# Side jobs of an attention loop in pieces over all its tiles, two quads of heads in one output bank, and a shorter count of chosen experts

## What is computed

```python
def attention(x):                       # 16 heads of 8
    q = x @ Wq;  latent = (x @ Wk + x @ Wv) @ W_down_kv          # latent: 32
    k = latent @ W_up_k;  v = latent @ W_up_v
    s = clip(q @ k.T / sqrt(128)) * exp(-1e-4 * abs(i - j))      # per head
    return (softmax(clip(s)) @ v) @ Wo
def experts(x):                         # 8 experts, the best 2 of each token, and a shared one
    top_logits, top_idx = top_k(x @ w_router, 2)
    moe = sum over the 2 chosen e: softmax(top_logits)[e] * (silu(proj_e) * gate_e) @ fc2_w[e],
          [proj_e, gate_e] = split(x @ fc1_w[e])
    return moe + (silu(x @ gate_w) * (x @ up_w)) @ down_w
x = layernorm(x + attention(x));  x = layernorm(x + experts(x))
```

## Time and profile before

| | us |
|---|---|
| median of 3 runs | 778.3 (775.71 to 781.35) |
| the profiled execution | 780.54 |
| its span, from first to last instruction | 778.4 |

### The profile page before, as it was taken

How to read it: one execution, slowest core, us unless ns; L and a number is a source line. 1 busy time by engine, 2 the same in 40 slices (tenths; PEclk the granted TensorE clock), 3 DMA queues, 4 the chain that set the end, 5 groups by cost and what they waited for, 6 DMA issues and landing times.

```text
span 778.4 us, 12970 instructions
## 1 busy us (share of the span) xinstructions
PE 658.6 (85%) x4815; PEld 296.5 (38%) x4815; DVE 316.5 (41%) x958; ACT 546.6 (70%) x634; POOL 281.0 (36%) x266
## 2 busy tenths in 40 slices
PE   5029899999999999999999998999999869958850
PEld 2013233333333333333333332333333869846530
DVE  1913332444334344433454442432435323236672
ACT  2028798998989899898889986899997224324222
POOL 1900450550333054033205643312101560267772
PEclk9658899999999999999899998999999989979995
DMA  3699564284255228425522855322243686873221
GB/s 114 214 326 395 190 218 174 96 297 176 96 190 187 99 101 311 157 95 190 189 82 96 314 194 195 131 82 96 100 145 119 204 247 195 265 217 101 67 73 49
DMA packets 76915, 132.04 MB, mean 170 GB/s; under 512 B 6512, under 2 KB 51888, under 8 KB 76848
## 3 DMA queue, kind: packets, MB, share of 16 engines
q1 hardware_dynamic: 72736, 123.63, 46.4%
q0 software_dynamic: 3584, 7.35, 3.1%
q10 hardware_dynamic: 528, 0.18, 0.1%
HBM read 82.38 MB, written 50.33 MB: 170 GB/s over the span
## 4 chain that ended last, share of the span: by engine, by line
PE 69%; DVE 11%; ACT 7%; DMA 4%; issue 3%; POOL 2%; another core or an unknown queue 1%; SPq 0%; ACTq 0%; DVEq 0%; POOLq 0%
PE ps L822 26%; PE ps L809 18%; ACT probs L704 7%; PE ps L980 5%; PE ps L764 5%; PE ps L975 4%; DVE ps L1288 3%; PE ps L989 2%; PE ps L844 2%; DMA queries<-stack_dram 2%; PE ps L868 1%; DVE small L1161 1%; DVE osb L1292 1%; PE ps L991 1%
## 5 line engine op out<-in xcount | busy, mean ns | idle before, releaser
L704 ACT ACTIVATE probs<-ps 128x1024 f32<-128x1024 f32 x512 | 482.4, 1038 | 94.2 <-DVE ps L1288 76.6
L822 PE MATMUL ps<-probs,V 128*9 128x512 f32 x2048 | 274.4, 609 | 0.8 <-ACT probs L704 0.5
L809 PE MATMUL ps<-queries,keys 32*128 32x512 f32 (+3 forms) x1408 | 194.5, 418 | 48.4 <-DMA queries<-stack_dram 31.9
L809 PEld LDWEIGHTS ps<-queries,keys 32*128 32x128 f32 x1408 | 95.0, 187 | 209.0 <-ACT probs L704 133.1
L1288 DVE TENSOR_TENSOR ps<-ps,cpk 128x256 f32<-128x256 f32 x256 | 101.8, 428 | 162.4 <-PE ps L809 154.6
L533 POOL TENSOR_TENSOR stage<-qk,rows_sb 128x512 fp32r<-128x512 f32 x28 | 36.8, 1315 | 169.0 <-DVE qk L1149 153.7
L573 POOL DMA_INDIRECT sorted_dram<-xn,slots x56 | 54.9, 980 | 73.2 <-ACT probs L704 35.5
L585 POOL DMA_INDIRECT queries<-result_dram,slots x56 | 57.3, 1023 | 45.4 <-PE ps L994 25.1
L733 ACT ACTIVATE probs<-ps 128x512 f32<-128x512 f32 x42 | 24.8, 599 | 40.4 <-PE ps L980 26.1
L822 PEld LDWEIGHTS ps<-probs,V 128*9 128x9 f32 x2048 | 30.5, 88 | 57.6 <-issue 43.2
L1391 DVE TENSOR_TENSOR probs<-probs,ps 128x512 f32<-128x512 f32 x42 | 28.4, 685 | 56.6 <-PE ps L975 16.3
(11 more groups left out here) (165 smaller groups left out, 586.2 us busy)
## 6 DMA issues: line engine op xcount, KB each, us to landing
stack_dram<-stage SPq DMA_DIRECT2D x64, 512.0 KB, 6.0
keys<-stack_dram SPq DMA_DIRECT2D x32, 1024.0 KB
queries<-stack_dram SPq DMA_DIRECT2D x32, 512.0 KB
keys<-expert_dram SPq DMA_DIRECT2D x36, 192.0 KB
sorted_dram<-y_pre SPq DMA_DIRECT2D x1, 4608.0 KB, 20.6
result_dram<-probs SPq DMA_DIRECT2D x18, 256.0 KB
rows_sb<-expert_dram SPq DMA_DIRECT2D x20, 192.0 KB
V<-expert_dram SPq DMA_DIRECT2D x16, 192.0 KB
```

Of the source, the lines that this page charges most:

```text
L704: nc.scalar.activation(probs[:, m % 3, 2 * j:2 * j + 2, :], ps[:, 2 * s:2 * s + 2, :], ACT.Exp, scale=SCALE).then_inc(exp_done, 1)
L809: last = mm(bank[2 * s + i][:, lo:hi], keys[rows, u, kt // CT, v, tok(kt % CT)], queries[rows, u, v, lo:hi], start=True, stop=True)
L822: last = mm(bank[OUT_BANK][32 * i:32 * i + HD + 1, :], V[:, c // 2 % 2, kt, 4 * (Q % QUADS) + i, :], probs[:, m % 3, i, :], start=(kt == 0 ...
```

## The change

`side_places` puts the jobs anew, over crossing tiles too, and a job can have one to four parts; each part does its share of the columns or of the 128-token tiles. One `o` job serves two quads, so there are two a chunk, and `evacuate` comes every 16 tiles. To make that possible V holds, for a pair of heads of two quads, `[v_a 1 | zeros | v_b 1]` of 9 columns each, and the outputs take 18 of these 27: the first quad of a pair adds zeros to the second's rows, and the second adds zeros to the first's. `quad(Q)` orders the quads 0, 2, 1, 3. The layer norm's statistics are in two steps (`aggregate` two tiles later). `cnt` takes running sums that VectorE makes (`choose`), with two matmuls instead of five. The other steps of the router follow `wo`, `lg` and `cnt` by a count of tiles.

```diff
             d, p = c - 1, c + 2
-            z = 0 if c % 2 else 4
-            places = {("xT", p): (0 if c % 2 else 2,), ("o", 4 * d + 3): (z + (1 if c % 2 else 0),),
-                      ("q", p): (z + 2, z + 3) if c % 2 else (z + 1, z + 2), ("a", d): (6 if c % 2 else 7,),
-                      ("k", p): (z + 8, z + 9), ("wo", d): (z + 10, z + 11), ("o", 4 * c): (z + 13,),
-                      ("x", d): (z + 16,), ("norm", p): (z + 17,), ("lg", d): (z + 18, z + 19), ("o", 4 * c + 1): (z + 21,),
-                      ("cnt", d): (z + 24,), ("v", p): (z + 25, z + 26), ("o", 4 * c + 2): (z + 27,)}
+            if c == NCH - 1:
+                places = {("o", 2 * d + 1): (1,), ("a", d): (4,), ("wo", d): (7, 8), ("x", d): (14,), ("lg", d): (16, 17),
+                          ("o", 2 * c): (18, 19), ("cnt", d): (22,)}
+            elif c % 2:
+                places = {("xT", p): (0,), ("o", 2 * d + 1): (1,), ("q", p): (4, 5, 6), ("a", d): (7, 8), ("k", p): (9,),
+                          ("wo", d): (13, 14), ("v", p): (15, 16), ("o", 2 * c): (19, 20), ("x", d): (22,),
+                          ("lg", d): (23, 24), ("norm", p): (26, 27), ("cnt", d): (29,)}
+            else:
+                places = {("o", 2 * d + 1): (1, 2), ("xT", p): (3, 4), ("q", p): (5,), ("a", d): (7, 8), ("k", p): (10, 11),
+                          ("wo", d): (12, 13), ("v", p): (16, 17, 18, 19), ("o", 2 * c): (20, 21), ("x", d): (23, 24),
+                          ("lg", d): (26,), ("norm", p): (27, 28), ("cnt", d): (30,)}
             if c == 0:
-                places.update({("norm", 0): (14,), ("norm", 1): (15,)})
+                places.update({("norm", 0): (13,), ("norm", 1): (14,)})
...
             def outputs(m):
                 Q, c, kt = m // NT, m // TPC, m % NT
+                half, k = Q % 2, quad(Q) % 2 * 4
...
-                if kt == 0 and Q:
-                    pe.wait_ge(o_evacuated, Q)
+                if kt == 0 and half == 0 and Q:
+                    pe.wait_ge(o_evacuated, Q // 2)
                 pe.wait_ge(exp_done, 2 * m + 2)
                 for i in range(4):
-                    last = mm(bank[OUT_BANK][32 * i:32 * i + HD + 1, :], V[:, c // 2 % 2, kt, 4 * (Q % QUADS) + i, :],
-                              probs[:, m % 3, i, :], start=(kt == 0), stop=(kt == NT - 1))
+                    last = mm(bank[OUT_BANK][32 * i:32 * i + 2 * (HD + 1), :],
+                              V[:, c // 2 % 2, kt, k + i, half * (HD + 1):(half + 2) * (HD + 1)], probs[:, m % 3, i, :],
+                              start=(kt == 0 and half == 0), stop=(kt == NT - 1 and half == 1))
...
                     elif what == "cnt":
-                        count_chosen(k)
+                        pe.wait_ge(chosen_ready, k + 1)
+                        mm(dst[:, 0:E], before, running[:, CT, :], start=True, stop=True)
+                        last = mm(dst[:, E:2 * E], all_ones, running[:, CT, :], start=True, stop=True)
...
             def keep_values(p, src):
-                rest(copy(V[:, p // 2 % 2, CT * (p % 2):CT * (p % 2 + 1), :, 0:HD],
-                          src.rearrange("r (t h d) -> r t h d", t=CT, h=HEADS)))
+                for half in range(2):
+                    rest(copy(V[:, p // 2 % 2, CT * (p % 2):CT * (p % 2 + 1), :, 2 * half * (HD + 1):2 * half * (HD + 1) + HD],
+                              src.rearrange("r (t w k d) -> r w t k d", t=CT, w=2, k=HEADS // 2)[:, half]))
...
             def choose(d):
-                tt(chosen[:, 0:CT, :], onehot[:, 0, d, :, :], onehot[:, 1, d, :, :], ALU.add).then_inc(chosen_ready, 1)
+                link(tt(running[:, 1:CT + 1, :], onehot[:, 0, d, :, :], onehot[:, 1, d, :, :], ALU.add))
+                for t in range(2, CT):
+                    link(tt(running[:, t, :], running[:, t, :], running[:, t - 1, :], ALU.add))
+                tt(running[:, CT, :], running[:, CT, :], running[:, CT - 1, :], ALU.add).then_inc(chosen_ready, 1)
...
-            def evacuate(Q):
-                dve.wait_ge(pv_done, NT * (Q + 1))
-                copy(osb[:, Q % 2, :], bank[OUT_BANK]).then_inc(o_evacuated, 1)
+            def evacuate(R):
+                dve.wait_ge(pv_done, 2 * NT * (R + 1))
+                copy(osb[:, R % 2, :], bank[OUT_BANK]).then_inc(o_evacuated, 1)
...
-                        statistics(y_pre[:, :], stats, mv, var, var_ready)
+                        for i in range(CT):
+                            rest(nc.vector.bn_stats(stats[:, i, :], y_pre[:, tok(i)]))
...
+                    if since["wo"] == 2:
+                        dve.wait_ge(dve_chain, links[0])
+                        aggregate(stats, mv, var, var_ready)
+                    if since["lg"] == 2:
+                        route_lanes(d)
+                    if since["lg"] == 3 and d < GROUP:
+                        choose(d)
```

More of the change, by code:

```diff
@@ L337, in block_kernel, with quad @@
         assert at[0] <= small.shape[1], at[0]
+        def quad(Q):
+            return (0, 2, 1, 3)[Q % QUADS]
         def stack_rows(n, p, i):
@@ L760, in _, with turn @@
             mm = nc.tensor.matmul
-            def turn(dst, src):
-                for t in range(CT):
+            def turn(dst, src, tiles=range(CT)):
+                for t in tiles:
                     last = nc.tensor.transpose(dst[:, tok(t)], src[:, tok(t)], ident)
@@ L896, in beside @@
                     what, k = name
-                    part = at_tiles.index(t)
-                    halves = range(2 * part, 2 * part + 2)
+                    part, n = at_tiles.index(t), len(at_tiles)
+                    tiles, cols = range(CT * part // n, CT * (part + 1) // n), slice(HALF * part // n, HALF * (part + 1) // n)
+                    dst = bank[SIDE_BANK] if part else side(name)
                     if what == "xT":
-                        turn_x(k)
+                        pe.wait_ge(x_loaded[k % 2], 16 * (k // 2 + 1))
+                        last = turn(dst, x_tok[:, k % 2, :], tiles)
@@ L901, in beside @@
                     elif what == "o":
-                        turn_output(side(name), k).then_inc(side_ready, 1)
-                    elif what in ("q", "k"):
-                        project(k, "qk".index(what), part)
+                        pe.wait_ge(o_evacuated, k + 1)
+                        last = turn(dst, osb[:, k % 2, :], tiles)
+                    elif what == "q":
+                        last = mm(dst[:, cols], Wq_sb[:, :], xT[:, k % 2, cols], start=True, stop=True)
+                    elif what == "k":
+                        last = mm(dst[:, cols], wfold[:, 2, :], xT[:, k % 2, cols], start=True, stop=True)
+                    elif what == "v":
+                        for i in tiles:
+                            last = mm(dst[:, tok(i)], xT[:, k % 2, tok(i)], wfold[:, 3, :], start=True, stop=True)
@@ L905, in beside @@
                     elif what == "a":
-                        turn(side(name), a_tok[:, k % 2, :]).then_inc(side_ready, 1)
+                        last = turn(dst, a_tok[:, k % 2, :], tiles)
                     elif what == "wo":
                         pe.wait_ge(s_wo, 32)
-                        last = out_project(bank[SIDE_BANK] if part else side(name), halves)
-                        if part:
-                            last.then_inc(side_ready, 1)
-                    elif what == "v":
-                        values(k, part)
+                        last = out_project(dst, tiles)
@@ L914, in beside @@
                     elif what == "x":
-                        dst = side(name)
                         pe.wait_ge(xn_ready, k + 1)
-                        turn(dst, xn[:, k, :]).then_inc(side_ready, 1)
+                        last = turn(dst, xn[:, k, :], tiles)
                     elif what == "norm":
-                        norms(k)
+                        pe.wait_ge(squared, k + 1)
+                        for i in range(2 * part // n, 2 * (part + 1) // n):
+                            last = mm(dst[32 * i:32 * i + 32, :], head_sum_h[:, :], squares[:, i, :], start=True, stop=True)
@@ L1168, in statistics @@
                 ts(v, m[:, :, 1], EPS, None, ALU.add).then_inc(s, 1)
+            def statistics(src, st, m, v, s, negated=None):
+                for t in range(CT):
+                    last = nc.vector.bn_stats(st[:, t, :], src[:, tok(t)])
+                link(last)
+                aggregate(st, m, v, s, negated)
             def normal_rows(dst, src, m, r):
```

126 lines of the change are left out of this document (48 added, 78 removed).

## The result

| | before | after |
|---|---|---|
| median, us | 778.66 (775.71 to 781.35) | 749.38 (748.8 to 752.01), 4 runs |
| ratio after / before, 95% | | 0.963 (0.960 to 0.966) |
| the profiled execution, us | 780.54 | 748.8 |
| its span, us | 778.4 | 746.7 |

The kernel is 3.7% faster: 29 us, where 39 were forecast. The same view by stretches as in the earlier trace rows, of the kernel after: chunks 0, 3, 4, 5, 6, then all after attention. The columns are the stretch and its length, the busy time of PE, PEld, DVE, ACT and POOL (with the instructions), the granted clock, the DMA share and GB/s.

What follows compares the result with a forecast made beforehand. ScalarE's exponentials set the free pace, with gaps where TensorE's or VectorE's side jobs delay them. Chunks summed to 498.8 us, plus 4.5 for wide outputs, 503.3 against 542.6: -39.3, so 739.0 us; own range 731 to 750, overall 722 to 762.

Steps and rivals of the forecast that it cites:

- Free pace and floor: Attention: ScalarE needs 0.917 us an exponential, 58.7 a chunk; a middle chunk of 67.8 loses 9.1 in gaps.
- 3.5 of losses: Odd chunks: waits expected to stay around side jobs and crossing tiles, 3.5 us on the floor, giving 62.2.
- TensorE's total of 57.7: TensorE's work in a chunk falls from 59.1 to about 57.7 us, under ScalarE's 58.7.
- Middle chunks: Odd chunks 1, 3, 5 take 62.2 us and even chunks 2, 4 take 62.0.
- The wider outputs, +4.5: Attention outputs: 18 columns of V for 9 cost 0.035 us in half of all tiles, +4.5 us.
- Chunk 0: Chunk 0 takes 67.0 us for 69.2, with the wait of about 4 us for the second `norm` kept.
- Queues that are moved past: GpSimd and SyncE behind `wo`: the next chunk's load goes out at 52 us and lands in time at 6.0.
- Instructions late again: Rival: VectorE's wait of 4.41 us comes again with half clock behind it, +6, 745 us; chance 0.12.
- Load late: Rival: the next chunk's load is 1.8 us late at three boundaries, +5.5, 745 us; chance 0.10.
- Crossing tiles cost more: Rival: pieces ahead of crossing scores cost 0.55 us each, not 0.25; +17, 756 us; chance 0.18.
- TensorE fits under: Rival: TensorE's total fits under ScalarE's and halves of the losses stay; -13, 726 us; chance 0.10.
- wide outputs slow: Rival: 18-column outputs lengthen tiles, at +0.25 us a tile 803 us, slower than before; chance 0.05.

Runs made afterwards that it cites:

- n_count5: `p_norm` with the count of chosen experts as before the change, five matmuls and one short VectorE operation instead of four; 736.43 us, ratio 0.947.
- o_stats: The changed kernel with every job in its old place and the aggregate straight behind `bn_stats` again; 766.45 us, ratio 0.985.
- p_wide32: `a_paced` with the outputs' stationary operand 32 columns wide instead of 18; 741.46 us, ratio 0.955.
- a_paced: The changed kernel with the first group's 32 row sends on GpSimd one a tile, from the start of chunk 6; 739.63 us, ratio 0.953.
- p_norm: `a_paced` with chunk 0's first two `norm` jobs at tiles 2 and 6 instead of 13 and 14; 734.27 us, ratio 0.944.
- a_again: The changed kernel run once more, unchanged; 747.54 us, ratio 0.963.
- b_burst: The kernel before the change with its row sends of chunks 5 and 6 no longer paced by the exponentials; 804.8 us, ratio 1.036.

## Why the prediction was right in part, point by point

The change is 29.3 us faster by the two medians; 39.3 was forecast. Of the 10.4 us between 749.38 and 739.0, 2.8 are how the two profiled executions lie in their runs (2.2 above the median before, 0.6 below it after); the spans account for the other 7.6 (746.7 for 739.1): chunks 5 and 6 +11.3, after attention +1.6, chunk 0 -1.1, the outputs' term -4.5, other chunks and rounding about +0.3. That 749.38 lies within the forecast's own range of 731 to 750 is luck: that range was made for wide outputs and for losses, and a stall that it did not hold filled it.

- **Free pace and floor.** Held for what it was used for: ScalarE's gaps were the loss, and they closed. The floor of 58.7 was not reached: the merged groups above give 60.5, 1.8 us more, and the gaps listed there add 1.5 where the sum had 3.5 of losses. The two errors met, so that the chunks came out right is luck in part.
- **TensorE's total of 57.7.** Its terms held where they have rows: turns gone, and the short count worth 0.65 a chunk against the 0.75 of the sum (`n_count5`).
- **Middle chunks.** 62.0 and 62.2 forecast; 61.72, 61.72, 62.42, 62.70 measured. The largest single losses named there, 1.37 at the end of a quad and 0.84 behind the statistics, went as said; the latter was costed at under 1 us a chunk and is worth 7.3 in all in the old places (`o_stats`): 0.6 in each of chunks 3, 5 and 7, where the clock stayed full, and 1.4 to 3.2 in the others of chunks 1 to 6, half-clock stretches in `o_stats` included.
- **The wider outputs, +4.5.** Mis-sized. The upper bound, 0.035 us a tile, was charged in half of the tiles. The loads grew by 4.1 us in all, even less than 256 x 0.035 = 9, and outputs from start to start stayed at 0.97 to 0.99; `p_wide32` adds 14 columns for 1.8 us by the medians, so nine cost about 1 (an estimate; no run has the change at 9 columns). The term should have been nothing to one. `a_paced` is the kernel that the sum described: its chunks add up to 500.4 where the sum had 498.8 without the term and 503.3 with it, and chunk 5's 63.65 for 62.2 is its largest miss. That its median of 739.63 meets the forecast's 739.0 owes something to this term's error, and to a before of 777.2 in its series where the forecast started from 778.3.
- **Chunk 0.** 65.90 for 67.0: the wait for the second `norm` stayed, as said. It was in reach all the time: 4.6 us by `p_norm`.
- **Queues that are moved past.** This is the step that failed. It followed what stands behind `wo` on GpSimd and SyncE, and not what stands behind `lg`: `gap_power` and, behind it, 12 sends whose gates were set for a `lg` at tiles 18 and 19. The step even gave the rule, to cost each queue that a job is moved past, and left one out. Chunks 5 and 6 were forecast at 122.9 and took 134.2; 124.2 with the sends apart.
- **Instructions late again (0.12, 745).** Its effect came, a stall of 6.3 us with a half clock behind it, above its price (10 us by the traces of after and `a_paced`, 8 by the medians of the pair, for 6). Its mechanism was wrong: not an accident that the change shifts, but a run of GpSimd's DMAs (`a_again`, `a_paced`, `b_burst`), behind which TensorE's signal is late and not VectorE's instruction. The wait of the earlier trace rows fits it (a late signal behind four sends 1.28 us apart, gone when the sends moved in `b_burst`), but no run takes those four sends apart alone.
- **Load late (0.10).** Came in small: at the end of chunk 0, 2.6 us in `a_paced`, and in after 1.01 us at the start of chunk 4 (TensorE's timeline above). It is not what made the miss.
- **Crossing tiles cost more (0.18), TensorE fits under (0.10), wide outputs slow (0.05).** None came: no fix wait near 0.5 in chunk 3, middle chunks at the forecast and not at 60, outputs at 0.98.

## What to carry to other kernels

When a job is moved, follow what stands behind it on every queue, down to DMA issues whose gates were tuned to the old place: a gate that has passed by the time the queue reaches it no longer spaces anything. Space small indirect DMAs over the work (one a tile of 1.83 us showed no wait here; 1.28 us apart they stalled the other engines), and read a wait with a "remote" releaser beside GpSimd's timeline of the same time before calling it chance. Even `p_norm` still makes its last 24 sends behind attention in runs of 5 to 7, and a "remote" wait of ScalarE of 4.93 us ends at 589.58, behind the last of them; no run here spaces those. A wait in one early chunk that the forecast accepts as given (here the second `norm`) is worth one look at whether its source can go earlier.

## What the hardware did that I had not expected

- Indirect DMAs from GpSimd issued 1.28 us apart delay TensorE's signals to VectorE and SyncE: ScalarE then stands for 2.4 to 3.3 us behind a run of 8, 5.5 and 6.2 in a run of 11, up to 16.6 in a run of 28 (VectorE's longest wait there is 17.1). At one a tile, about 1.83 us, `a_paced` had none in chunks 5 to 7. VectorE's signal to ScalarE and ScalarE's to TensorE came in under 0.1 us at the stall in after. It happens with the sends alone on the DMA engines (52 GB/s) and with a load beside them (394). The cause inside the chip is open.
- The half clock at such a stall lasted 13.7 us in after for a stall of 6.3, and 10.2 in `a_again` for one of 5.6; in after, chunks 5 and 6 were 10.0 us longer than with the sends apart, so that about 3.7 came on top of the wait.
- Widening a stationary operand from 9 to 32 columns costs 20 ns in each load, but only some 3 us in 2048 loads (1.8 by the medians for the last 14 columns, the estimate of 1 for the first 9), with 512 columns streaming behind each.
